# The attention's output product made transposed, and the tail that used to turn its sum

## The reference, cut to what matters

```python
o = jnp.einsum('bhqk,bkhd->bqhd', probs, v_all)
o = o.reshape(bsz, seqlen, HQ * D)
return jnp.einsum('bse,de->bsd', o, Wo)          # attention's result
...
logits = x_flat @ gate_w.T + expert_bias
base_out = jnp.einsum('bth,oh->bto', x, W_up)
z = jnp.einsum('nh,erh->ner', x_flat, lora_A)    # x, x_flat: attention's result
```

## Time and profile before

| | us |
|---|---|
| median of three runs | 3247.13 |
| the profiled execution, own time | 3248.76 |
| its span, first to last instruction | 3246.8 |
| PE busy | 3034.6 (93%) |
| PE weight loads busy | 2022.1 (62%) |
| DVE busy | 1556.9 (48%) |
| ACT busy | 1293.1 (40%) |
| POOL busy | 1532.6 (47%) |

### The profile page before, as it was taken

The page is one execution under the profiler, slowest core; times in us unless marked ns, Lnnn a source line. Parts: engine busy times, 40 slices in busy tenths (PEclk is TensorE's granted clock), DMA queues, the critical chain, the costliest instruction groups (busy, mean ns, idle before and its releaser), DMA issues. The chain is left out here.

```text
span 3246.8 us, 55910 instructions
## 1 busy us (share of the span) xinstructions
PE 3034.6 (93%) x15256; PEld 2022.1 (62%) x15264; DVE 1556.9 (48%) x3931; ACT 1293.1 (40%) x3014; POOL 1532.6 (47%) x1323
## 2 busy tenths in 40 slices
PE   3799999999999999999999999999999986888887
PEld 2466666666666666666666666666666664555454
DVE  6544444444444444444444444444444444556555
ACT  1344444444444444444444444444444431222221
POOL 7355555555555555555555555555555520001000
PEclk9899999999999999999999999999999997999898
DMA  8544444434443444545444444344444443112110
GB/s 294 192 122 123 117 117 117 118 117 118 117 118 117 118 118 125 189 123 176 124 119 120 119 120 121 118 127 123 126 118 123 123 148 100 31 37 53 32 30 13
DMA packets 416196, 378.26 MB, mean 117 GB/s; under 512 B 83427, under 2 KB 347763, under 8 KB 414996
## 3 DMA queue, kind: packets, MB, share of 16 engines
q1 hardware_dynamic: 358484, 186.81, 20.2%
q0 software_dynamic: 50480, 174.40, 17.2%
q10 hardware_dynamic: 7056, 14.46, 1.2%
HBM read 341.23 MB, written 25.85 MB: 113 GB/s over the span
## 5 line engine op out<-in xcount | busy, mean ns | idle before, releaser
L533 DVE CUSTOM_DVE_ANT_0 ps_s<-ps_s,mask 128x544 f32<-128x544 f32 x512 | 374.9, 732 | 938.8 <-PE ps_s L360 929.2
L262 POOL DMA_INDIRECT v_sb<-in_v_rows_w,v_row x504 | 488.3, 969 | 469.3 <-PE ps_oT L385 258.7
L319 PE MATMUL ps_t<-wqkv,xT 128*128 128x512 f32 x1488 | 704.1, 596 | 0.0
L383 PEld LDWEIGHTS ps_oT<-pT,v_sb 128*128 128x128 f32 x4096 | 527.0, 192 | 186.6 <-issue 186.1
L433 ACT ACTIVATE ps_s<-ps_s,nmax 128x544 f32<-128x544 f32 x512 | 352.3, 688 | 628.9 <-DVE nmax L533 627.8
L383 PE MATMUL ps_oT<-pT,v_sb 128*128 128x128 f32 x4096 | 541.3, 275 | 9.8 <-issue 9.8
L343 PE MATMUL ps_t<-wo,oT 128*128 128x512 f32 x1024 | 524.8, 597 | 2.5 <-ACT oT L448 0.9
L359 PE MATMUL ps_s<-k_sb,qT 128*128 128x416 f32 x1024 | 446.9, 518 | 19.2 <-issue 15.2
L543 DVE TENSOR_SCALAR p_sb<-ps_s,rinv 128x544 f32<-128x544 f32 x512 | 401.3, 784 | 23.9 <-DVE rinv L540 0.3
L448 ACT ACTIVATE oT<-ps_oT 128x128 f32<-128x128 f32 x512 | 141.9, 277 | 637.0 <-PE ps_oT L385 634.3
L368 PEld LDWEIGHTS ps_pT<-ident_sb,p_sb 128*128 128x128 f32 x2048 | 251.3, 141 | 188.3 <-issue 185.4
(11 more groups left out here) (216 smaller groups left out, 3775.4 us busy)
## 6 DMA issues: line engine op xcount, KB each, us to landing
k_sb<-in_kT SPq DMA_DIRECT2D x2048, 64.0 KB
v_sb<-in_v_rows_w,v_row POOLq DMA_INDIRECT x512
v_new<-v_raw SPq DMA_DIRECT2D x128, 64.0 KB, 3.3
wo<-in_wo_w POOLq DMA_DIRECT2D x2, 4096.0 KB, 15.3
y_scratch<-y_sb SPq DMA_DIRECT2D x32, 256.0 KB, 2.1
xT<-x1T_scratch POOLq DMA_DIRECT2D x31, 256.0 KB, 4.6
tab<-rope_scratch POOLq DMA_DIRECT2D x31, 256.0 KB, 4.7
wqkv<-in_wqkv_w ACTq DMA_DIRECT2D x6, 1024.0 KB, 10.6
```

The costliest lines, as they stand in the source:

```text
L262: e.indirect_dma_start(out=v_sb[:, b % 2, c, :], out_offset=None, in_=A["v_rows_w"], in_offset=bass.IndirectOffsetOnAxis(ap=v_row[:, b, c: ...
L319: m = e.matmul(ps_t[bank_of(t)][:, :], xT[:, k, :], wqkv[:, k, 512 * t:512 * t + 512], start=k == 0, stop=k == KC - 1)
L383: e.matmul(ps_oT[:, :], v_sb[:, b % 2, c, h * D:(h + 1) * D], pT[:, u % 2, c, :], start=c == 0, stop=False)
L533: e.tensor_tensor_reduce(out=scores(u), in0=scores(u), in1=mask[:, b % 2, :], scale=-SCALE, scalar=3e38, op0=ALU.add, op1=ALU.min, accum_o ...
```

## The change

In `out_product` the roles are exchanged: the four 128 x 128 parts of a head's `wo` are stationary one after another, and `oT` of the head (128 tokens) moves through each. The bank then holds features (in four chunks) by tokens, and so do `y_sb`, `y_d`, `a` and `yin`. In the tail DVE therefore writes the sum straight into `xT`; the transposes on the PE, the copies on ACT and two semaphores go. The bytes that ACT copies, SP stores and SP loads are as many as before.

```diff
                 for h in range(h0, h1):
-                    m = e.matmul(ps_t[0][:, :], oT[:, i, h, :], wo[:, h, :], start=h == 0, stop=h == HQH - 1)
+                    for c in range(KC):
+                        m = e.matmul(ps_t[0][:, c * P:(c + 1) * P], wo[:, h, c * P:(c + 1) * P], oT[:, i, h, :], start=h == 0 and c == 0, stop=h == HQH - 1 and c == KC - 1)
...
             def head(k):
 
                 for p in both:
-                    turn4(k, p, a, "a_sum", "a_turned")
-                for p in both:
-                    e.wait_ge(event["a_copied"], 2 * k + p + 1)
+                    e.wait_ge(event["a_sum"], 2 * k + p + 1)
                     product(k, p, gz, E1 + E1 * R1, 2)
                     product(k, p, wup, HID, 3, stop=False).then_inc(event["base"], 1)
...
-            def head(k):
-                for p in both:
-                    copy(k, p, xT[p][:, :, :], four(bank[p][0]), "a_turned", "a_copied")
-
...
-                if more:
-                    head(k + 1)
...
-            head(0)
...
-                    e.tensor_tensor(a[p][:, :], a[p][:, :], yin[p][:, :], ALU.add).then_inc(event["a_sum"], 1)
+                    e.tensor_tensor(xT[p][:, :, :], a[p][:, :].rearrange("p (k n) -> p k n", k=KC), yin[p][:, :].rearrange("p (k n) -> p k n", k=KC), ALU.add).then_inc(event["a_sum"], 1)
```

More of the change, by code:

```diff
@@ L1083, in tail @@
     event = {n: sem("c_" + n) for n in (
-        "a_sum", "a_turned", "a_copied", "base", "z_masked", "z_turned", "z_copied", "delta", "x2_ready", "x2_turned", "x2_copied",
+        "a_sum", "base", "z_masked", "z_turned", "z_copied", "delta", "x2_ready", "x2_turned", "x2_copied",
         "xr_done", "xr_masked", "c_done", "c_copied", "t_done", "t_split",
```

## The result

The changed kernel takes **3308.32 us** (median of 4 runs, 3304.56 to 3312.24), the kernel before on the same occasion 3245.99 (4 runs, 3241.43 to 3252.37). The ratio is 1.0191, with a 95% interval of 1.0169 to 1.0212: slower by 62 us, where 4.6 were forecast and 3260 was the end of the range. The profiled execution took 3308.93 us, its span is 3306.6.

What follows compares the result with a forecast made beforehand. The PE's own instructions were taken to bound attention, the order of work the tail; +16 - 9.4 + 0 - 2 = +4.6 us on a median of 3247.13 gave 3251.7 us, range 3242 to 3260.

Steps and rivals of the forecast that it cites:

- The output product, +16 us: In attention, eight narrow records at 0.893 us replace two wide at 0.862 us a head, over 512 heads.
- cheap records: Rival: the output product's eight records go at the transposes' beat, +5 us, total 3240.7 us; chance 0.12.
- a stall at each stationary group: Rival: the output product stalls at each change of stationary group, as in L1179, +65 us, total 3301 us; chance 0.05.
- The sustained 81 ns against 131 ns: Skill's load-and-matmul pairs at 128 and 512 columns; would add an estimated 650 us over the kernel; put aside.
- The tail, -9.4 and -2: Last stage: head starts 1.34 us earlier in 7 steps, -9.4 us; milder clock restarts at L1208, -2 us.
- the alternation: In the tail, L1208's twelve records alternate between 6.57 and 7.74 us; a step 1.34 us shorter must break that.
- The first head, 0: The tail's first head could start some 4 us earlier but waits for a weight's transfer and conversion: zero gain.
- All of it lies on the path: In attention, the output product's added 16 us count in full; other engines wait longer only by this amount.
- my sum: Whole kernel: +16 - 9.4 + 0 - 2 = +4.6 us, giving 3251.7 us, 0.14% more.
- no change: Whole kernel: a result within 0.2% (6.5 us) of the kernel before, given chance 0.55.
- The PE's waits for issue ahead of L359: In attention, PE standstills of some 25 us before L359 and L383, put down to issue, not another engine.

Runs made afterwards that it cites:

- g1_after: The changed kernel unaltered, run again on the same chip as three padded versions: 3275.48 us, ratio 1.0117 to the kernel before.
- g4_pad64: The changed kernel with 64 semaphore increments that do nothing ahead of TensorE's later code, attention's included: 3255.89 us, ratio 1.0062 to the kernel before.
- h2_before_pad64: The kernel before with 64 increments of an unused semaphore at the start of TensorE's attention code: 3265.1 us, ratio 1.0076 to the kernel before.
- h4_after: The changed kernel unaltered, one run on a later occasion to look at its signals: 3295.88 us.
- the first and third group: Sets of follow-up runs: the first tried edits separately and 32 idle instructions (1.0056), the third 64 in the kernel before (1.0076) and an earlier tail turning (0.9995).
- i2_after: The changed kernel unaltered, timed again on an occasion with late signals: 3296.85 us, ratio 1.0176 to the kernel before.
- h3_early_turn: The kernel before with its wide output product, the tail's halves added by GpSimd and turned a step earlier: 3236.44 us, ratio 0.9995 to the kernel before.

## Why the prediction was wrong

- *The output product, +16 us*: right. 0.893 for 0.862 us a head was read correctly off L383, and attention's records take 16.1 us more. The rivals of cheap records and of a stall at each stationary group are refuted by the 0.89; that the latter's 3301 us lies near the measured time is chance. The sustained 81 ns against 131 ns of the Trainium skill (TensorE: Matmul & The Clock Gate, Part 2, "Back-to-back issue gap"), which I had put aside, does not hold for these records either, which follow at 0.112 and 0.431 us.
- *The tail, -9.4 and -2*: the sum is right, -11.3 for -11.4. From the closing products to the A-matrix product a step saves 1.45 us instead of 1.34, which is 10.2 over seven, and the clock gave the rest, 1.1 for 2. That the two errors cancel is luck. As argued, the alternation broke: the steps are 64.8 to 65.2 us from the second on, where they were 66.0 and 67.1 by turns, and L1207 settles between the two kinds of restart in the earlier trace rows (7.19 us at 2879).
- *The first head, 0*: right, shown by the longer wait for `qwb`.
- **The step that failed is "All of it lies on the path. The order is unchanged, so no other engine waits longer for anything except by this amount".** I priced the duration of 3072 more records and took their order for all else that counts. Their *code* also has a length and so a place, and their signals can come late where another engine needs them at once. No rival had either. Of the 60.5 us of lost time in the first profile, 25.1 are lost in g1_after too, without late signals, and 35.4 are not. 24 to 26 us of the 62 are the second stops at five jumps with the half clock behind them (72.6 less 48.7, 98.1 less 72.2); they are shown from both sides, by g4_pad64 and by h2_before_pad64. From g1_after to g4_pad64 it is 11.3 us of stops ahead of L361 and about as much of half clock.
- Without late signals and without the second stops, as in g4_pad64, the change still costs 0.62% by the ratio, 0.41% at its lower end, where my sum gives 0.14%. The profile of g4_pad64 agrees with the sum (span 3250.9, where 3246.8 and 4.6 make 3251.4; lost time 48.7 for 47.5), but the median times differ by 17 us (3255.9, 3238.7). Some 10 us of that I can place in no row: the two profiles compared are single executions of kernels whose times spread by 7 and 15 us, and the stage ahead of attention alone varies by 10 over the profiles. This stays open. By its own interval the change is slower than the 0.2% that I had called no change, even at this place of the code.
- The remaining 17 to 35 us (89.9 and 108.0 of h4_after and the first profile, less the 72.6 of g1_after) are the late signals. That they exist depends on the occasion: of six, three had them, and two of the six (the first and third group) were on the same chip, without and with them. That they cost something depends on the kernel: with widths of 512 and 256 the attention loses little by them. Why the signal of the turned probabilities is the one delayed beside four narrow products is **not** settled, nor what delays any. In the first measurement after's profile has late signals; before's has none, but it is of another execution than the four of the ratio, so whether these had them is not known. It matters little, as before's times do not move with them. The ratios with both measured among late signals are 1.0176 (i2_after) and, without, 1.0117 to 1.0139.
- In the earlier trace rows there was a sign that I read past. The PE's waits for issue ahead of L359, 15.2 us in 10 times, I took for a small remainder. Ten is the number of jumps back of the two attention loops, and each stop says that an instruction was not there yet. Had I asked what those ten were, an estimate would have followed for any edit that lengthens TensorE's code: ten more stops as long as the longest in that row, 2.2 us, are 22 us, and the range should have reached that far.

No version here beats the kernel before: the fastest that computes everything is h3_early_turn, and its interval includes 1.

## What to carry to other kernels

Where a profile shows an engine waiting for "issue" at each jump back of a loop, an edit that changes the number of that engine's instructions can move the price of each jump by microseconds, for better or worse. Before blaming or praising such an edit, time it again with a few dozen idle instructions ahead of the loop, and give before the same treatment. And compare an edit's ratio on more than one occasion if other engines idle for "remote": the same code was 1.2% or 1.9% slower. If the instruction queue moves no packet around a jump that has no stop and one at each jump that has, it is the fetch that the engine waits for.

## What the runs showed of the hardware

- A shift of TensorE's code by 64 instructions moves a kernel of 3.2 ms by 20 to 28 us, in either direction (3275.5 to 3255.9; 3237.3 to 3265.1); one of 256 leaves the stops as they are (3275.5 to 3280.5).
- The stops at a loop's jump go with packets of the instruction queue: nine jumps without a packet, in three executions, are nine without a stop.
- Behind each of after's five second stops (2.0 to 2.5 us) the granted clock was at 1.2 GHz for 6.8 us: 0.72 over 12 us at the first. Behind g4_pad64's single stop of 1.7 us it stayed at 2.4 GHz, 1.00; behind its next one, of 2.0 us, it did not, 0.86 in 1899 to 1911 us.
- TensorE's signals reached DVE and ACT up to 4.0 us late (3.7 in after, 4.0 in h2_before_pad64) on some occasions, 79 to 176 times in an execution without those of the scores.
- A small DVE operation that overlaps a GpSimd addition of 128x512 (1.27 us) can be stretched several times: a cast of 0.22 us to as much as 0.97 us, an addition of 0.28 us to 1.19 us.
